# State-space stage: five state buffers, C rows in pairs, the exponential in halves, projections on other steps

## The reference

```
x, z    = split(h @ in_proj_w.T)
xc      = silu(conv4(x) + conv_b)
dt,B,C  = split(xc @ x_proj_w.T)
dt      = softplus(dt @ dt_proj_w.T + dt_proj_b)
per token: hst = exp(dt*A) * hst + (dt*xc)*B ;  y = sum over n of hst*C
out     = ((y + D*xc) * silu(z)) @ out_proj_w.T
```

## Time and profile before

| what | before |
|---|---|
| median of three runs | 3325.3 us |
| the profiled execution, its own time | 3331.51 us |
| its span, first to last instruction | 3329.7 us |
| the stage, from its first load to its last scans | 1566 to 2760 us |
| its eight blocks of 16 steps | 1660 to 2755 us |
| the first scans of the eight blocks start near | 1662, 1799, 1940, 2078, 2215, 2352, 2492, 2630 us |

### The profile page before, as it was taken

How to read it: one execution, slowest core, us unless ns; L and a number is a source line. 1 busy time by engine, 2 the same in 40 slices (tenths; PEclk the granted TensorE clock), 3 DMA queues, 4 the chain that set the end, 5 groups by cost and what they waited for, 6 DMA issues and landing times. The chain is left out here.

```text
span 3329.7 us, 36467 instructions
## 1 busy us (share of the span) xinstructions
PE 2674.7 (80%) x12202; PEld 1820.2 (55%) x12202; DVE 1977.3 (59%) x3556; ACT 1053.3 (32%) x1637; POOL 1380.7 (41%) x865
## 2 busy tenths in 40 slices
PE   6555389956899999997477987879779676997998
PEld 2222156645799999996133433434334233665997
DVE  8999868645122222222788888999889894332111
ACT  4544222200111111111345545455454430221111
POOL 0000034426333333332058687686786852112332
PEclk8777699965899999998688998999889887998999
DMA  3000100011899999986200000101001000115996
GB/s 109 0 0 0 43 7 19 13 31 30 297 328 323 323 328 326 318 310 219 103 26 26 30 34 26 39 26 39 26 26 38 26 26 22 36 42 202 349 349 235
DMA packets 90565, 395.04 MB, mean 119 GB/s; under 512 B 20854, under 2 KB 48006, under 8 KB 63840
## 3 DMA queue, kind: packets, MB, share of 16 engines
q1 hardware_dynamic: 68864, 351.46, 30.0%
q0 software_dynamic: 21600, 42.37, 3.6%
HBM read 364.94 MB, written 39.29 MB: 121 GB/s over the span
## 5 line engine op out<-in xcount | busy, mean ns | idle before, releaser
L1240 POOL TENSOR_TENSOR ss_h<-ss_h,ss_cs 128x2048 f32<-128x2048 f32 x128 | 578.9, 4524 | 84.4 <-DVE ss_h L1603 76.6
L1320 PE MATMUL ss_y<-ss_h,all_ident 128*128 128x512 f32 x1024 | 528.3, 665 | 39.0 <-POOL ss_h L1240 39.0
L1095 DVE TENSOR_TENSOR experts_in<-experts_sil,experts_pU 128x512 f32<-128x512 f32 x176 | 121.0, 687 | 638.7 <-PE experts_pU L1039 638.7
L1603 DVE TENSOR_TENSOR_SCAN ss_h<-ss_da,ss_c_h,ss_dbu 128x512 f32<-128x512 f32 x384 | 470.7, 1268 | 38.9 <-ACT ss_da L1460 32.2
L1320 PEld LDWEIGHTS ss_y<-ss_h,all_ident 128*128 128x128 f32 x1024 | 216.8, 215 | 316.1 <-issue 266.6
L1460 ACT ACTIVATE ss_da<-ss_dt,ss_decay 128x512 f32<-128x512 f32 x512 | 326.5, 711 | 152.8 <-POOL ss_dt L1220 94.0
L1596 DVE TENSOR_TENSOR ss_dbu<-ss_dtx,ss_bB 128x1024 f32<-128x1024 f32 x256 | 314.5, 1229 | 62.2 <-PE ss_bB L1310 34.2
L1039 PE MATMUL experts_pG<-experts_xt,experts_wa 128*128 128x128 f32 x2816 | 346.7, 277 | 2.5 <-DMA experts_wa<-in_w_all 1.9
L1039 PE MATMUL experts_pU<-experts_xt,experts_wa 128*128 128x128 f32 x2816 | 344.2, 275 | 0.0
L1039 PEld LDWEIGHTS experts_pG<-experts_xt,experts_wa 128*128 128x128 f32 x2816 | 331.6, 193 | 3.6 <-issue 2.6
L1048 PE MATMUL experts_pY<-experts_wa,experts_in 128*128 128x256 f32 x1408 | 332.7, 379 | 0.0
(11 more groups left out here) (322 smaller groups left out, 3794.7 us busy)
## 6 DMA issues: line engine op xcount, KB each, us to landing
experts_wa<-in_w_all SPq DMA_DIRECT2D x176, 1536.0 KB, 9.1
ss_cs<-ss_c_rows SPq DMA_DIRECT2D x32, 1024.0 KB, 4.6
moe_rows<-route_xn SPq DMA_DIRECT2D x16, 512.0 KB, 3.1
all_x<-in_x SPq DMA_DIRECT2D x8, 512.0 KB, 9.2
gf_xb<-in_x SPq DMA_DIRECT2D x8, 512.0 KB, 3.8
ss_h<-moe_ys SPq DMA_DIRECT2D x4, 1024.0 KB, 6.9
moe_rows<-all_x SPq DMA_DIRECT2D x8, 512.0 KB, 3.3
experts_xr<-moe_rows,moe_token POOLq DMA_INDIRECT x176, 7.7
```

The lines of the kernel that those rows point to most:

```text
L1095: nc.vector.tensor_tensor(IN[t.two][:].rearrange("p f t -> p (f t)"), SIL[t.two][:], pU[t.two][:], ALU.mult)\
L1240: pool.tensor_tensor(h[:], h[:], CS[q % 2][:, n % GROUP].unsqueeze(1).to_broadcast([P, CI, BT]), ALU.mult)\
L1320: mm = pe.matmul(y[:, c], ident[:], H[n % RING][:, c], start=(n == 0), stop=(n == N - 1))
L1603: ins = V.tensor_tensor_scan(H[n % RING][:, c], DA[n % 2][:, c], DBU[:, c % 2], first, ALU.mult, ALU.add)
```

## The change

It does six things. The ring of state tiles gets a fifth buffer and is indexed by the running step number. The C rows come in groups of two, in one tile of four rows. ACT's exponential is done in halves at steps 9 and 10, its logarithm moves from step 11 (behind `decays(b, 12)`) to step 10. POOL's `low_part` and `step_size` move one step earlier, to 9 to 12. POOL's `gate` moves ahead of the wait of step 2. The x projections go to the steps 1, 2, 4 and 5, the out projections to 3 and 6.

```diff
-    RING = 4
-    GROUP = 4
+    RING = 5
+    GROUP = 2
+    AHEAD = 2
...
-        DA, CS = two("da", [P, CI, BT]), two("cs", [P, GROUP, BT])
+        DA = [m_.sb(f"da{b}", [P, CI, BT]) for b in range(AHEAD)]
+        CSB = m_.sb("cs", [P, 2 * GROUP, BT])
+        CS = [CSB[:, h * GROUP:(h + 1) * GROUP] for h in range(2)]
...
+        X_STEPS = (1, 2, 4, 5)
... load_group
-                        wait(sp, "added", (RING + n + 1) * TPB)
+                        wait(sp, "added", (RING + 1) * TPB)
... low_part (POOL), and first_steps (DVE) with half + 1
-                    wait(pool, "exp_done", b + 1)
+                    wait(pool, "exp_done", b * 2 + half + 1)
... the loop of POOL
+                        if tail and n == 2:
+                            gate(b - 1)
                         wait(pool, "scanned", (b * N + n + 1) * 2)
-                        h = H[n % RING]
+                        h = H[(b * N + n) % RING]
...
-                        if tail and n == 2:
-                            gate(b - 1)
-                        if prep and n in (10, 11):
-                            low_part(b + 1, n - 10)
-                        if prep and n in (12, 13):
-                            step_size(b + 1, n - 12)
+                        if prep and n in (9, 10):
+                            low_part(b + 1, n - 9)
+                        if prep and n in (11, 12):
+                            step_size(b + 1, n - 11)
... x_part (PE)
                         wait(pe, "xb_done", b * CI + c)
+                        if c == 2 and b > 1:
+                            wait(pe, "out_done", (b - 2) * 2 + 1)
... out_part (PE)
                     if half == 0:
                         wait(pe, "yz_done", b * CI + CI)
                         if b < NB - 2:
-                            wait(pe, "xb_done", (b + 3) * CI)
+                            wait(pe, "xb_done", (b + 2) * CI + 2)
...
                     else:
                         wait(pe, "out_done", b * 2 + 1)
+                        if b < NB - 2:
+                            wait(pe, "xb_done", (b + 3) * CI)
... the loop of PE
-                        if prep and n in (1, 2, 3, 4):
-                            x_part(b + 1, n - 1)
-                        if tail and n in (5, 6):
-                            out_part(b - 1, n - 5)
+                        if prep and n in X_STEPS:
+                            x_part(b + 1, X_STEPS.index(n))
+                        if tail and n in (3, 6):
+                            out_part(b - 1, n // 6)
... (convolve in the same way)
... ACT
-                def exponential(b):
-                    wait(act, "u_done", b * CI + CI)
-                    A_(DTX[b % 2][:], DTX[b % 2][:], ACT.Exp, scale=-1.0).then_inc(s["exp_done"], 1)
+                def exponential(b, half):
+                    e = DTX[b % 2][:, 2 * half:2 * half + 2]
+                    wait(act, "u_done", b * CI + 2 * half + 2)
+                    A_(e, e, ACT.Exp, scale=-1.0).then_inc(s["exp_done"], 1)
... decays
-                    wait(act, "scanned", (b * N + n - 1) * 2)
+                    k = b * N + n
+                    wait(act, "scanned", (k - AHEAD + 1) * 2)
+                    if k < AHEAD:
+                        wait(act, "added", (RING + 2 + k) * TPB)
... the loop of ACT
-                        if prep and n in (2, 3, 4, 5):
-                            copy_x(b + 1, n - 2)
+                        if prep and n - 1 in X_STEPS:
+                            copy_x(b + 1, X_STEPS.index(n - 1))
... (copy_conv in the same way)
                         if prep and n in (9, 10):
                             copy_dt(b + 1, 2 * n - 17)
+                            exponential(b + 1, n - 9)
                         if prep and n in (8, 9):
                             copy_dt(b + 1, 2 * n - 16)
                         if prep and n == 10:
-                            exponential(b + 1)
-                        if prep and n == 11:
                             logarithm(b + 1)
... the loop of DVE
-                        if tail and n in (6, 7):
-                            add_out(b - 1, n - 6)
+                        if tail and n in (4, 7):
+                            add_out(b - 1, n // 7)
```

More of the change, by code:

```diff
@@ L1129, in state_space @@
         ZS, LN1 = m_.sb("zs", [P, CI, BT]), XR[:, :, TAPS - 1:]
-        DA, CS = two("da", [P, CI, BT]), two("cs", [P, GROUP, BT])
+        DA = [m_.sb(f"da{b}", [P, CI, BT]) for b in range(AHEAD)]
+        CSB = m_.sb("cs", [P, 2 * GROUP, BT])
+        CS = [CSB[:, h * GROUP:(h + 1) * GROUP] for h in range(2)]
         H = [m_.sb(f"h{b}", [P, CI, BT]) for b in range(RING)]
-        Y = [b[:].rearrange("p a t -> p (a t)").rearrange("p (j k d) -> p j k d", k=r.K, d=D) for b in H + CS + DA]
+        Y = [b[:].rearrange("p a t -> p (a t)").rearrange("p (j k d) -> p j k d", k=r.K, d=D) for b in H + [CSB] + DA]
         ROWS, BC2 = m_.sb("rows", [64, BT]), m_.sb("bc2", [P, BT], BF16)
@@ L1184, in load_group @@
                     if n < 2:
-                        wait(sp, "added", (RING + n + 1) * TPB)
-                    sp.dma_start(CS[n % 2][:].rearrange("p n t -> p (n t)"),
+                        wait(sp, "added", (RING + 1) * TPB)
+                    sp.dma_start(CS[n % 2].rearrange("p n t -> p (n t)"),
                                  c_rows[b, k * GROUP:(k + 1) * GROUP].rearrange("n t -> (n t)").partition_broadcast(P))\
@@ L1319, in add_up @@
                     for c in range(CI):
-                        mm = pe.matmul(y[:, c], ident[:], H[n % RING][:, c], start=(n == 0), stop=(n == N - 1))
+                        mm = pe.matmul(y[:, c], ident[:], H[(b * N + n) % RING][:, c], start=(n == 0), stop=(n == N - 1))
                     mm.then_inc(s["summed"], 1)
@@ L1373, in _ @@
                             add_up(b - 1, n + N - 2)
-                        if prep and n in (1, 2, 3, 4):
-                            convolve(b + 1, n - 1)
+                        if prep and n in X_STEPS:
+                            convolve(b + 1, X_STEPS.index(n))
                         if prep and n == 0:
@@ L1436, in copy_dt @@
                     A_(DT[b % 2][:, c], q, ACT.Relu, bias=dt_b[:, c:c + 1]).then_inc(s["u_done"], 1)
-                def exponential(b):
-                    wait(act, "u_done", b * CI + CI)
-                    A_(DTX[b % 2][:], DTX[b % 2][:], ACT.Exp, scale=-1.0).then_inc(s["exp_done"], 1)
+                def exponential(b, half):
+                    e = DTX[b % 2][:, 2 * half:2 * half + 2]
+                    wait(act, "u_done", b * CI + 2 * half + 2)
+                    A_(e, e, ACT.Exp, scale=-1.0).then_inc(s["exp_done"], 1)
                 def logarithm(b):
-                    wait(act, "exp_done", b + 1)
+                    wait(act, "exp_done", b * 2 + 2)
                     wait(act, "dt_done", b * 2)
@@ L1457, in decays @@
                     wait(act, "dt_done", b * 2 + 2)
-                    wait(act, "scanned", (b * N + n - 1) * 2)
+                    k = b * N + n
+                    wait(act, "scanned", (k - AHEAD + 1) * 2)
+                    if k < AHEAD:
+                        wait(act, "added", (RING + 2 + k) * TPB)
                     for c in range(CI):
-                        ins = A_(DA[n % 2][:, c], DT[b % 2][:, c], ACT.Exp, scale=DECAY[:, c, n:n + 1])
+                        ins = A_(DA[k % AHEAD][:, c], DT[b % 2][:, c], ACT.Exp, scale=DECAY[:, c, n:n + 1])
                     ins.then_inc(s["da_done"], 1)
@@ L1473, in _ @@
                     copy_dt(0, c)
-                exponential(0)
+                exponential(0, 0)
+                exponential(0, 1)
                 logarithm(0)
-                wait(act, "added", (RING + 3) * TPB)
                 decays(0, 0)
@@ L1482, in _ @@
                             normalise(b + 1)
-                        if prep and n in (2, 3, 4, 5):
-                            copy_x(b + 1, n - 2)
+                        if prep and n - 1 in X_STEPS:
+                            copy_x(b + 1, X_STEPS.index(n - 1))
                         if prep and n == 8:
                             copy_bc(b + 1)
-                        if b == 0 and n == 0:
-                            wait(act, "added", NB * TPB)
                         if n < N - 1:
@@ L1493, in _ @@
                             copy_ht(b + 1, 1)
-                        if prep and n in (2, 3, 4, 5):
-                            copy_conv(b + 1, n - 2)
+                        if prep and n - 1 in X_STEPS:
+                            copy_conv(b + 1, X_STEPS.index(n - 1))
                         if prep and n == 6:
@@ L1554, in first_steps @@
                         e, u = DTX[0][:, part], DT[0][:, part]
-                        wait(dve, "exp_done", 1)
+                        wait(dve, "exp_done", half + 1)
                         ch.link(V.tensor_scalar(REST, e, 1.0, 1.0, ALU.add, ALU.subtract))
@@ L1602, in half_step @@
```

(2 more changed lines are left out.)

## The result

The changed kernel takes 3283.8 us (median of four, 3280.7 to 3284.9) beside 3326.2 for the kernel before on the same chip: ratio 0.9872, 95% interval 0.9855 to 0.9889. The forecast was 3291, the range 3278 to 3311.

The account below looks back on a forecast made before the run. DVE was taken as the busiest engine, its waits for decays at block boundaries as the main loss. Boundary 26 plus x steps 8 less ACT 0.3 gave 34 us, from 3325.3 to 3291; range 3278 to 3311.

Parts of the forecast that it names:

- The boundary: Between blocks, POOL's dt one step earlier ends DVE's waits for decays; late additions still delay spreads; gain 26.0 us.
- a sign of being wrong: At block boundaries: the prediction is wrong if DVE still waits 4 us or more, for whomever.
- The x steps: PE's x and out projections in new order: 5 us in blocks 1 to 6, block 0 included 8.
- ACT: Logarithm and two table changes ahead of step 12's decays: DVE waits 0 to 1.0 us, 0.3 in the sum.
- rival 4: On ACT, a table change costs 2.6 us instead of 1.3 in the new place: 3294; chance 0.03.
- Five buffers: State ring: the fourth buffer is always free in time, so a fifth brings no gain and no cost.
- Groups of two: C row loads: 64 transfers of half size, covered by two products' time of at least 9.3 us; no cost.
- The gate: POOL's four multiplications moved into its wait for state 2: no cost; uncovered, 5 us on POOL once a block.
- The halves: ACT's exponential: its first half needs only two of four chunks, letting POOL's train start earlier; no separate size.
- 1, PE at the lower clock takes the boundary over: Late additions at block boundaries all last 7.20 us: 3303, or 3311 with nothing from the x steps; chance 0.17.
- 2, slow x steps: PE's x steps at half clock last about 17 us instead of 9; one in each of seven blocks: 3350; chance 0.07.
- 3: POOL's train is held, for instance by late C rows; the boundary wait only changes its name: 3325; chance 0.05.

Follow-up runs that it names:

- run 6: The changed kernel with the last additions of a block moved back by one step of PE: 3270.9 us, ratio 0.9833.
- run 1: The changed kernel with four state buffers and C rows in groups of four, as before: 3288.3 us, ratio 0.9883.
- run 9: The kernel before with the first decays' wait for the experts' outputs put behind their wait for dt: 3341.4 us beside 3344.2, ratio 0.9995.
- run 2: The kernel before with only the new x and out projection steps and the early gate: 3315.2 us, ratio 0.9964.
- run 5: The changed kernel with POOL's gate back behind the product of step 2: 3320.1 us, ratio 0.9974.
- run 10: The changed kernel itself measured again, in another set of runs: 3302.0 us beside 3344.2 for the kernel before, ratio 0.9879.
- run 7: The changed kernel with the late additions moved back one step, but four state buffers and groups of four: 3309.7 us, ratio 0.9946.
- run 3: The kernel before with only the halved exponential, logarithm at 10, and low part and step size one step earlier: 3304.3 us, ratio 0.9937.
- run 4: The changed kernel with the exponential whole again at step 10, POOL's first low part waiting for it: 3319.0 us, ratio 0.9976.

## Why the prediction was right, step by step

- **The boundary.** Forecast: 39.7 us of waits go, 13.7 come, 26.0. Traced: 41.6 to 13.4, 28.2. The 41.6 include 2.1 at step 2, where DVE waited for the last addition, which I had left out. What comes is of the kind forecast, a spread behind a late addition (run 6), and its sum is right for this trace. The places are not: the forecast had product 12 in time for step 0 and only product 13 late. About half of what came stands at step 0, behind product 12, whose addition took 6.51 and not 5.40 in the boundary shown. The boundary behind block 1, which was to cost nothing, cost 2.0, and three that were to cost 1.9 cost 0.7 to 1.2. So the sum agrees in part by luck. Its size isn't a property of the kernel either, since another trace has 6.7 and pays at step 11. The first boundary, with 1.7 and 2.7, is over the 4 us that the forecast named as a sign of being wrong; the other six have 0.7 to 3.6.
- **The x steps.** Forecast 8, traced 10.8. Blocks 1 to 6 gave 5.2 for the 5. Block 0 gave 5.6 for the 3 (7.8 to 2.2). The convolution in its first x step shows the clock: eight passes in 3.70 in the change, 5.45 before and 5.91 in run 1.

```profile
1673.13 3.70 PE L1286 MATMUL ss_q<-ss_xr,ss_tap 128*128 128x512 f32 x8 [0.69 <-ACT ss_xr L1421]
```

```profile
1678.40 5.45 PE L1280 MATMUL ss_q<-ss_xr,ss_tap 128*128 128x512 f32 x8 [0.69 <-ACT ss_xr L1413]
```

  All the traces fall in two groups (small gaps left in). With the old order of steps, block 0 waits 8.4 to 8.6 at steps 3 to 8 where this convolution took 5.4 to 5.7, and 5.9 where it took 3.70 (run 9). With the new order it waits 4.9 to 5.3 where it took 5.5 to 5.9 (runs 1, 2, 5), and 2.3 to 2.6 where it took 3.70. So the order is worth some 3 at either clock, as forecast, and the other 2.5 are the clock's.
- **What the forecast lacked.** 1.5 at the first scan (run 9) and 1.7 at steps 9 to 11, which come and go. Less 0.7 more at steps 12 to 15, and with the two above, that is 28.2 + 10.8 + 1.5 + 1.7 - 0.7 = 41.5 of waits, and 42.4 in the medians. The term that was furthest off is the x steps', by the clock of block 0.
- **ACT.** Forecast 0.3. DVE's waits for decays at step 12 are 0.2 and 0.3, in two blocks. In the second trace (run 10) they are 1.6 in four blocks, each behind a wait at step 11, which is over the 1.0 allowed. One of ACT's changes of function table, in the changed kernel:

```profile
2011.54 1.28 ACT L1454 ACT_TABLE_LOAD   x1
2012.83 1.91 ACT L1454 ACTIVATE ss_xr<-ss_dtx 128x2048 f32<-128x2048 f32 x1
```

  1.29 us from load to use, as in the earlier trace rows; a change of 2.66 us (the Trainium skill, ScalarE: Activation LUTs, What ACT_TABLE_LOAD costs) isn't seen here, and rival 4 is out.
- **Edits costed at nothing.** Five buffers: right as far as runs tell (run 1), for the reason given, which run 7 shows from the other side: once the addition stands behind the spread, the buffer counts. Groups of two: the loads land in 3.5 us and nobody waits for them. The gate: hidden as forecast, but "uncovered it would be 5 us on POOL" was the wrong price. Uncovered, DVE pays 2.0 to 4.4 in seven blocks for the out projection alone, 23 us, and the kernel is 36 slower (run 5). The prediction had it as a detail. Without it the out projection at step 3 costs more than the new order of x and out steps brings: 3320.1, beside 3304.3 for run 3, which has neither.
- **The halves.** Named as what lets the train start, rightly, but not priced: 35 us (run 4).
- **Rivals.** 1, PE at the lower clock takes the boundary over: it does so in part, by 13.4 us, where the forecast's own sum had 13.7. 2, slow x steps: of those whose spreads were recorded the longest lasted 10.1, and 1.1 of that was a wait for DVE. 3 is out: the rows of C land in 3.5 us and the wait for decays is gone.

The wait at step 11 goes with PE's clock. The thirteen traces have 104 blocks. In the 27 that have this wait, of 1.0 to 3.2 us, the granted clock over DVE's step 10 was 0.65 to 0.68; in the other 77 it was 0.72 or more. What stays open is why the clock is low through step 10 in some blocks and not in others. Between two traces of one program it moved, and no run here controls it.

## What to carry to other kernels

When a wait is removed, look at what stands in the same engine's list behind the work that is now late: here a spread behind an addition, and putting them in the other order was worth 13 us more, once the spare buffer let it (runs 6 and 7). Price a moved instruction not by its own length but by the one that waits for it at the new place. An edit that is worth nothing alone (the gate 1.0004, the buffer within noise) can be what another needs (the kernels without them are 36 and 39 us slower), so it is tested by taking it out of the full kernel and not only by adding it to the old one.

## What the runs showed of the hardware

- Of the two waits ahead of ACT's first decays, the one written first rides on the instruction and the other stands alone ahead of the load of the function table, in both orders that were run. In the order of before, the wait for dt stood alone and the load, 1.28 us, was exposed behind it. The other order hides it (run 9).
- One program laid its waits differently in two traces with nearly the same sum (34.6 and 34.9).
- The same kernel took 3327 and 3344 us in two sets of runs, and the 17 us lay ahead of the stage studied (1055.0 beside 1054.7 us for its blocks). So times are compared only within a set.
